# A two-layer gated attention and experts kernel: the second attention's tables loaded with x, its DRAM zeroed inside the first attention, its output weights prepared inside the slots, and a shorter row of steps for the normalization constants

## The chip, the cores and the metric

One Trainium2 chip, one of its cores. The metric is the device time of one execution in microseconds (us), median over several executions.

## The reference

The state `x` has 64 batches of 128 tokens by 128 features; the context `ctx_1024` has 64 batches of 77 tokens. Four stages are added to `x` in turn, each on a layer-normalized `x`:

```python
x = x + tanh(g_xattn[0]) * L0_xattn(ctx, ctx, layernorm(x))   # feature maps exp(z), exp(-z); 16 heads
x = x + tanh(g_ffn[0])   * L0_ffn(layernorm(x))               # 8 gated experts of width 336, routed
x = x + tanh(g_xattn[1]) * L1_xattn(layernorm(x), ctx, ctx)   # attention with relative key and value tables
x = x + tanh(g_ffn[1])   * L1_ffn(layernorm(x))               # 8 experts of width 256, top 2
# layernorm(x) = (x - mean) / sqrt(var + 1e-5)
# L1_xattn: q = x Wq + bq, k = c Wk + bk, v = c Wv + bv, 16 heads of 8
#   scores = (q k + q rel_key[q - k]) / sqrt(8); p = softmax(scores)
#   out = (p v + p rel_value[q - k]) Wo + bo
```

All of `x` stays in SBUF (`x_all`, 128 partitions by 64 batches by 128) from the load to the last stage.

## The kernel before

The program is a row of blocks, and all engines meet at a barrier between two blocks: the load of `x` (`load_x`, L129), normalization constants (`layernorm_constants`, L82), the first attention (`feature_attention`, L167), constants, router and scores, the first experts, constants (the third call), the second attention (`relative_attention`, L1384), constants, router, scores and the second experts.

`load_x`: SP issues four DMAs of 1 MB for `x`, then the small tables of both routers (L144). POOL first clears those router tables (L150). DVE takes `bn_stats` of every batch as its quarter lands (L164).

`layernorm_constants` turns the two half-row statistics of all 64 batches into mean, `1/sqrt(var + eps)` and, where asked, the shift `-mean * rstd`. It is called four times. DVE runs a chain in which `link` (L101 to L105) lets every operation wait for the one before it: seven operations (L108 to L116), of which the sixth releases the square root on ACT (L95), then the reciprocal (L118), four operations of one Newton step (L120 to L123) and the shift (L125).

Both attentions are software pipelines, and `slots` (L66) gives each engine the same slot numbers: the first and last slots are written out, the middle ones are a hardware loop over two parities. In a slot an engine runs a hand-ordered row of functions that belong to different batches, each with its own semaphore waits.

First attention, SP (L239 to L251): seven weight tables; then in slot n the DMA of batch n's context (`xc`, L246), which PE's `prep_z` (L269) needs. At slot 2, behind the context of batch 2, SP also issues the 20 DMAs of the first experts' weights (`stage_cuts`, L249, some 4 MB). Batch 3's context follows them in the same queue.

Second attention: SP loads eight tables (L1476), waits until POOL has cleared `q_pos` (L1761), and writes these zeros into the two DRAM buffers `queries` (L1479), because later only a diagonal pattern of them is written (L1485) and the whole is read back (L1492). SP waits until both have landed before its first slot.

DVE copies the identity into head order (`by_head_ident`, L1800), waits for the eight tables, and prepares: the selector and the split row bias (L1804 to L1812, six steps of `bias_split`), the output weights and bias times the gate (L1814, L1815; `weights_ready` 1 and 2), the masked key table (L1817), then the low part of the output weights and the output bias in rows (L1821 to L1831). The bias takes one product on PE (L1650). ACT first waits for the tables and for `weights_ready` 1 and rounds the output weights (L1661). Only then do the slots begin on PE and ACT, and on DVE after L1831. PE waits for `weights_ready` 3, `w_out_low`, `table_ready` and `bias_split` 6 ahead of its first slot; POOL waits for `weights_ready` 3.

The slots run from -4. Batch 0 comes up like this: ACT normalizes (L1693), PE transposes (L1522), ACT rounds (L1667), DVE makes the low part (`low_xn`, L1837), PE projects in slot -2 (L1526, L1542), ACT and DVE split the queries (L1684, L1686, L1845, L1847; the count `proj_low`), POOL spreads them over the heads (`mask_queries`, L1769), SP writes them to DRAM and reads them back, and PE computes scores (L1557, L1559).

## Time and profile before

| | us |
|---|---|
| median of 3 executions | 2190.94 (2188.76 to 2191.07) |
| the profiled execution | 2186.11 |
| its span in the profile | 2184.2 |
| load and first constants | 0 to 25.1 |
| first attention, to its last statistics | 25.65 to 466.3 |
| second constants to the end of the first experts | 467.2 to 1195.3 |
| third constants | 1195.6 to 1199.5 |
| second attention | 1199.97 to 1785.3 |
| fourth constants | 1785.6 to 1789.3 |
| second router and experts | 1789.8 to 2184.2 |

Busy time as a share of the span: PE 93%, DVE 87%, ACT 72%, POOL 72%. A timeline row gives the start, the length (for merged rows the stretch they cover), the engine ("SPq" is a DMA issue on SP, "PEld" a weight load), the line, the operation and the count; behind it, in brackets, how long the engine had been idle and what released it. The last column but two of a windows row is TensorE's granted clock (1.00 is 2.4 GHz, 0.50 is 1.2 GHz), the last two are the DMA engines' busy share and GB/s.

### The profile page before, as it was taken

The numbers are of one execution on the slowest core, as the hardware profiler recorded it, in microseconds if no ns is written. First come the engines' busy times: TensorE is split into PE (matmuls) and PEld (weight loads), VectorE is DVE, ScalarE is ACT, GpSimd is POOL, SyncE is SP. The second block draws the span as 40 slices with busy tenths as digits, with TensorE's granted clock in tenths as the row PEclk, the third lists the DMA queues.
The fourth block names the chain that finished last, engine by engine and source line by source line (L and its number), as shares of the span: only waits on it lengthen the run. The fifth ranks groups of instructions, "written<-read, shape, count | busy, mean of one in ns | idle before, by whom it ended". The sixth has DMA issues, their size and how long they took to land. (4 is left out here: it accounts for less than half of the span.)

```text
span 2184.2 us, 82970 instructions
## 1 busy us (share of the span) xinstructions
PE 2035.4 (93%) x28380; PEld 1568.6 (72%) x28380; DVE 1904.4 (87%) x4327; ACT 1570.4 (72%) x3516; POOL 1575.8 (72%) x1457
## 2 busy tenths in 40 slices
PE   3999999977999999999998799999999966999999
PEld 2788888854666666666665689999999944666666
DVE  5899999987888888888888689999999968888888
ACT  3788888875565655555555578888888756888887
POOL 1576777743666666666665789999999933888887
PEclk9999999987999999999999799999999978999999
DMA  5000000002432222222220455555555520000000
GB/s 155 14 6 7 6 7 6 7 2 74 102 90 82 78 86 82 82 85 83 79 84 16 85 81 89 82 89 82 89 83 89 83 60 1 15 10 14 10 14 15
DMA packets 476443, 121.41 MB, mean 56 GB/s; under 512 B 431879, under 2 KB 446855, under 8 KB 475604
## 3 DMA queue, kind: packets, MB, share of 16 engines
q1 hardware_dynamic: 476084, 120.41, 25.2%
q8 instruction: 42, 0.69, 0.1%
q14 instruction: 29, 0.24, 0.0%
q10 hardware_dynamic: 288, 0.07, 0.0%
HBM read 106.51 MB, written 13.89 MB: 55 GB/s over the span
## 5 line engine op out<-in xcount | busy, mean ns | idle before, releaser
L1220 POOL TENSOR_TENSOR f_low<-f_hidden,f_high 128x512 f16<-128x512 f32 x336 | 442.4, 1322 | 217.9 <-ACT f_high L1152 216.0
L1178 DVE TENSOR_TENSOR f_hidden<-f_hidden,f_share 128x512 f32<-128x512 f32 x336 | 374.2, 1114 | 0.0
L1367 POOL TENSOR_TENSOR f_low<-f_hidden,f_high 128x512 f16<-128x512 f32 x256 | 296.7, 1160 | 74.1 <-ACT f_high L1310 74.1
L1158 ACT ACTIVATE f_act_out<-f_gate 128x512 f32<-128x512 f32 x336 | 200.5, 597 | 193.2 <-PE f_gate L1122 193.1
L1201 DVE SCALAR_TENSOR_TENSOR f_hidden<-f_up,f_act_out 128x512 f32<-128x512 f32 x336 | 229.8, 684 | 83.2 <-PE f_up L1122 51.0
L1152 ACT ACTIVATE f_high<-f_hidden 128x512 f16<-128x512 f32 x336 | 210.5, 626 | 72.9 <-DVE f_hidden L1178 71.6
L1132 PE MATMUL f_y<-w_high,f_high 128*128 128x128 f16 x1344 | 243.3, 219 | 2.0 <-POOL f_low L1220 2.0
L1769 POOL TENSOR_TENSOR a_q_head_high<-a_q_t_high,a_head_mask 128x2048 f16<-128x2048 f16 x64 | 233.0, 3641 | 16.3 <-DVE a_q_t_low L1847 8.0
L1132 PE MATMUL f_y<-w_high,f_low 128*128 128x128 f16 x1344 | 243.4, 219 | 0.0
L1132 PE MATMUL f_y<-w_low,f_high 128*128 128x128 f16 x1344 | 243.3, 219 | 0.0
L1769 POOL TENSOR_TENSOR a_q_head_low<-a_q_t_low,a_head_mask 128x2048 f16<-128x2048 f16 x64 | 233.0, 3641 | 0.0
L1353 DVE SCALAR_TENSOR_TENSOR f_hidden<-f_in,f_act_out 128x512 f32<-128x512 f32 x256 | 175.8, 687 | 49.7 <-ACT f_act_out L1317 49.7
L1317 ACT ACTIVATE f_act_out<-f_in 128x512 f32<-128x512 f32 x256 | 152.9, 597 | 65.4 <-PE f_in L1279 59.6
L1557 PE MATMUL a_score<-a_k_t_high,a_q_head_high 128*128 128x77 f16 x1024 | 186.4, 201 | 4.8 <-POOL a_q_head_low L1769 2.8
L1291 PE MATMUL f_y<-w_high,f_high 128*128 128x128 f16 x1024 | 184.8, 219 | 2.3 <-DVE x_all L1331 0.6
L1559 PE MATMUL a_score<-table_low,a_q_pos 128*128 128x77 f16 x1024 | 186.7, 202 | 0.0
L1559 PE MATMUL a_score<-table_high,a_q_pos 128*128 128x77 f16 x1024 | 186.6, 202 | 0.0
L1557 PE MATMUL a_score<-a_k_t_high,a_q_head_low 128*128 128x77 f16 x1024 | 186.4, 201 | 0.0
L1557 PE MATMUL a_score<-a_k_t_low,a_q_head_high 128*128 128x77 f16 x1024 | 186.2, 201 | 0.0
L1291 PE MATMUL f_y<-w_high,f_low 128*128 128x128 f16 x1024 | 184.6, 219 | 0.0
L1291 PE MATMUL f_y<-w_low,f_high 128*128 128x128 f16 x1024 | 184.6, 219 | 0.0
L1878 DVE TENSOR_TENSOR a_prob_t_low<-a_trans,a_prob_t_high 77x512 f16<-77x512 f32 x256 | 166.6, 670 | 15.1 <-ACT a_prob_t_high L1706 14.3
(280 smaller groups left out, 8171.1 us busy)
## 6 DMA issues: line engine op xcount, KB each, us to landing
f_share<-expert_shares SPq DMA_DIRECT2D x128, 256.0 KB, 3.1
a_q_pos<-queries SPq DMA_DIRECT2D x64, 512.0 KB
f_share<-expert_shares SPq DMA_DIRECT2D x128, 128.0 KB, 3.0
relative_values<-a_rel_all SPq DMA_DIRECT2D x512, 8.0 KB
x_all<-in_x SPq DMA_DIRECT2D x4, 1024.0 KB, 8.0
f_share<-expert_shares SPq DMA_DIRECT2D x128, 32.0 KB, 1.8
queries<-a_q_parts SPq DMA_DIRECT2D x64, 64.0 KB, 3.1
a_rel<-relative_values SPq DMA_DIRECT2D x64, 64.0 KB, 2.1
```

The costliest lines, as they stand in the source:

```text
L1132: mm = nc.tensor.matmul(dst, h[r][:, own], w_down[part][:, m, :], start=(m == 0 and t == 0 and k == 0), stop=(m == M - 1 and k == 2), skip ...
L1152: nc.scalar.activation(high[r][:, :], hidden[r][:, :], ACT.Copy).then_inc(high_ready, 1)
L1158: nc.scalar.activation(act_out[m % RING][:, :], gate_ps[m % BANKS][:, :], ACT.Silu, scale=1.0 / WSCALE).then_inc(act_ready, 1)
L1178: nc.vector.tensor_tensor(hidden[r][:, :], hidden[r][:, :], share[k][:, :, :].rearrange("p t q -> p (t q)"), ALU.mult).then_inc(scaled, 1)
L1201: nc.vector.scalar_tensor_tensor(out=hidden[r][:, :], in0=up_ps[m % BANKS][:, :], scalar=1.0 / WSCALE, in1=act_out[r][:, :], op0=ALU.mult, ...
L1220: nc.gpsimd.tensor_tensor(low[r][:, :], hidden[r][:, :], high[r][:, :], ALU.subtract).then_inc(low_ready, 1)
L1291: mm = nc.tensor.matmul(dst, h[m % RING][:, own], w_down[part][:, m, :], start=(c == 0 and t == 0 and k == 0), stop=(c == per - 1 and k == 2),
L1353: nc.vector.scalar_tensor_tensor(out=dst, in0=src, scalar=scalar, in1=a, op0=op, op1=ALU.mult).then_inc(hidden_ready, 1)
L1367: nc.gpsimd.tensor_tensor(low[k][:, :], hidden[k][:, :], high[k][:, :], ALU.subtract).then_inc(low_ready, 1)
L1557: nc.tensor.matmul(dst, q[:, QC * g:QC * (g + 1), :], t[:, :], start=(k == 0), stop=False)
L1559: mm = nc.tensor.matmul(dst, q_pos[p][:, g, :], key_table[k][:, 0, window], start=False, stop=(k == 1))
L1769: nc.gpsimd.tensor_tensor(q_head[p][k][:, :, :], q_t[p][k][:, :].unsqueeze(2).broadcast_to([P, P, NH]), head_mask[:, :].unsqueeze(1).broad ...
```

## The change

1. `layernorm_constants`: operations that do not need each other no longer wait for each other; eps is added together with the square; the Newton step takes three operations in place of four.
2. A class `AttentionTables` is allocated with the router tables. Its eight tables are loaded by SP at the end of `load_x`; POOL clears one row `empty_row` (256 bytes a partition) there.
3. The two DRAM buffers are zeroed in the first attention: SP issues both DMAs at slot 2, behind the experts' weights, with `empty_row` repeated 16 times as their source. `q_pos` is no longer cleared.
4. In the second attention all engines wait for the long-landed tables only. The product for the output bias goes to PE's slot -2 (its head), the rounded output weights to ACT's slot -2 (its head), and the seven DVE operations L1821 to L1831 to the head of DVE's slot -1. PE's waits move to the first place that needs each.

```diff
 layernorm_constants, DVE
-  link(mean = half1 + half4); link(diff = half1 - half4); link(var = half2 + half5)
-  link(diff = (diff * 0.25) * diff); link(var = var / D + diff); link(var = var + EPS)   # 6: releases ACT
-  link(mean = mean * 0.5)
+  diff = half1 - half4; var = half2 + half5; mean = half1 + half4
+  dve.wait_ge(step, 1)
+  diff = (diff * 0.25 * D) * diff
+  dve.wait_ge(step, 4)
+  var = (var + EPS * D) + diff
+  dve.wait_ge(step, 5)
+  var = var * (1.0 / D)                                                                  # 6: releases ACT
+  mean = mean * 0.5
   dve.wait_ge(root, 1)
   rstd = reciprocal(sd)
-  link(newton = rstd * rstd); link(newton = newton * var); link(newton = newton * -0.5 + 1.5)
-  link(rstd = rstd * newton)
+  newton = (rstd * -0.5) * rstd; newton = newton * var; rstd = (newton + 1.5) * rstd      # each waits
```

(The block above writes the operations in short; the ones below are the diff's own lines.)

```diff
 load_x
-                sp.wait_ge(cleared, sum(len(r.zeros) for r in routers))
-                for r in routers:
+                sp.wait_ge(cleared, sum(len(r.zeros) for r in (*routers, attention)))
+                for r in (*routers, attention):
                     for t, src in r.loads:
                         sp.dma_start(t, src).then_inc(r.loaded, 16)
 feature_attention, SP
                     if isinstance(n, int) and n == 2:
                         for dst, src in stage_cuts:
                             sp.dma_start(dst, src).then_inc(stage_in, 16)
+                        empty = attention.empty_row[:, :].unsqueeze(1).broadcast_to([P, QG, QC * NH])
+                        for dst in attention.q_read:
+                            sp.dma_start(dst, empty).then_inc(attention.emptied, 16)
 relative_attention, SP
-                for t, src in WEIGHTS:
-                    sp.dma_start(t[:, :], io[src]).then_inc(weights_in, 16)
-                sp.wait_ge(cleared, 1)
-                for p in range(2):
-                    sp.dma_start(q_read[p], q_pos[p][:, :, :]).then_inc(q_zeroed, 16)
-                sp.wait_ge(q_zeroed, 32)
+                sp.wait_ge(attention.emptied, 32)
 relative_attention, PE
+                        if isinstance(n, int) and n == -2:     # in project
+                            pe.wait_ge(bias_split, 6)
+                    if isinstance(n, int) and n == -2:         # head of slot
+                        output_bias()
-                pe.wait_ge(weights_ready, 2)
-                nc.tensor.matmul(fin_ps[:, 0:D], b_v[:, :], w_o[:, :], start=True, stop=True).then_inc(bias_ready, 1)
-                pe.wait_ge(weights_ready, 3)
-                pe.wait_ge(w_out_low, 1)
-                pe.wait_ge(table_ready, 1)
-                pe.wait_ge(bias_split, 6)
+                def output_bias():
+                    pe.wait_ge(weights_ready, 2)
+                    nc.tensor.matmul(fin_ps[:, 0:D], b_v[:, :], w_o[:, :], start=True, stop=True).then_inc(bias_ready, 1)
+                pe.wait_ge(attention.loaded, 16 * len(attention.loads))
                 slots(pe, FIRST, LO, HI, LAST, slot)
 relative_attention, ACT
-                act.wait_ge(weights_in, 16 * len(WEIGHTS))
-                act.wait_ge(weights_ready, 1)
-                nc.scalar.activation(w_out[0][:, :], w_o[:, :], ACT.Copy).then_inc(w_out_high, 1)
+                act.wait_ge(attention.loaded, 16 * len(attention.loads))
+                    if isinstance(n, int) and n == -2:         # head of slot
+                        high_output()
 relative_attention, POOL
-                    last = nc.gpsimd.memset(q_pos[p][:, :, :], 0.0)
-                last.then_inc(cleared, 1)
-                pool.wait_ge(weights_ready, 3)
+                pool.wait_ge(attention.loaded, 16 * len(attention.loads))
 relative_attention, DVE
-                dve.wait_ge(weights_in, 16 * len(WEIGHTS))
+                dve.wait_ge(attention.loaded, 16 * len(attention.loads))
...
+                    if isinstance(n, int) and n == -1:         # head of slot; L1821 to L1831
+                        output_tables()
```

The remaining waits of PE go to the first users: `table_ready` to `scores(0)`, `weights_ready` 3 to `mix_turn(0)`, `w_out_low` to `fin_project(0)`. The DRAM tensors and their access patterns move into `AttentionTables` unchanged.

## Rows read from the trace of the kernel before

**Rows 1.** Windows: the loop of the second attention, busy us by engine, clock, DMA share, GB/s

```profile
1219.00:1780.00 561.00, 542.50 (x12711) 517.11 (x12711) 500.48 (x1397) 444.74 (x1267) 509.37 (x253) 0.98 0.52 82
```

**Rows 2.** Timeline, third call of layernorm_constants: start us, us, engine, line, operation

```profile
1195.60 1.28 ACT L95 ACT_TABLE_LOAD   x1 [4.89 <-PEq L1097]
1195.63 0.27 DVE L108 TENSOR_TENSOR mean<-stats 128x64 f32<-128x64 f32 x1 [0.30 <-PEq L1097]
...
1196.55 0.23 DVE L111 SCALAR_TENSOR_TENSOR ln_diff<-ln_diff 128x64 f32<-128x64 f32 x1
...
1197.07 0.20 DVE L115 TENSOR_SCALAR ln_var<-ln_var 128x64 f32<-128x64 f32 x1
...
1197.30 0.26 ACT L95 ACTIVATE ln_sd<-ln_var 128x64 f32<-128x64 f32 x1 [0.41 <-DVE ln_var L115]
...
1198.25 0.23 DVE L120 TENSOR_TENSOR ln_newton<-rstd 128x64 f32<-128x64 f32 x1
...
1199.00 0.22 DVE L123 TENSOR_TENSOR rstd<-rstd,ln_newton 128x64 f32<-128x64 f32 x1
```

**Rows 3.** Timeline, DVE at the start of the first attention: two operations without a wait

```profile
30.59 0.43 DVE L498 TENSOR_TENSOR a_fm_w<-a_w_rep,a_w_sign 128x256 f32<-128x256 f32 x1 [5.44 <-DMA a_fc_w<-in_fc_w]
30.93 0.15 DVE L502 TENSOR_TENSOR a_own_mask<-a_head_mask 128x4 f32<-128x4 f32 x1
```

**Rows 4.** Timeline, start of the second attention, all engines

```profile
1200.01 4.20 DVE L1800 COPY a_by_head_ident<-ident 128x128 f32<-128x128 f32 x1 [0.54 <-PEq L91]
...
1200.28 1.80 POOL L1761 MEMSET a_q_pos<- 128x2048 f16 x1
...
1202.33 1.80 POOL L1761 MEMSET a_q_pos<- 128x2048 f16 x1
...
1205.31 0.29 DVE L1804 TENSOR_TENSOR a_sel<-ident 128x128 f16<-128x128 f32 x1 [1.09 <-DMA a_high_rows<-in_high_rows]
...
1207.09 0.27 DVE L1817 TENSOR_SCALAR table_low<-table_low,a_high_rows 128x197 f16<-128x197 f16 x1
...
1207.22 0.79 PE L1650 MATMUL a_mix<-a_w_o,a_b_v 128*128 128x128 f32 x2 [13.53 <-DVE a_b_o L1815]
1207.29 0.86 ACT L1693 ACTIVATE a_xn<-x_all,xn_shift,rstd 128x128 f32<-128x128 f32 x2
...
1208.40 0.47 PE L1522 MATMUL a_prep<-ident,a_xn 128*128 128x128 f32 x1 [0.38 <-DVE a_b_o L1823]
...
1209.55 0.28 DVE L1837 TENSOR_TENSOR a_xt_low<-a_prep,a_xt_high 128x128 f16<-128x128 f32 x1
...
1209.90 0.29 PE L1526 MATMUL a_prep<-a_xt_high,table_high 128*128 128x128 f16 x1 [1.02 <-DVE a_xt_low L1837]
```

**Rows 5.** Timeline, POOL and DVE in the first slots of the second attention

```profile
1212.13 3.64 POOL L1769 TENSOR_TENSOR a_q_head_high<-a_q_t_high,a_head_mask 128x2048 f16<-128x2048 f16 x1 [8.00 <-DVE a_q_t_low L1847]
...
1215.28 0.29 DVE L1845 TENSOR_TENSOR a_q_parts<-a_prep,a_q_parts 128x128 f16<-128x128 f32 x1 [2.07 <-ACT a_q_t_high L1686]
```

**Rows 6.** Timeline of the first attention, SP's queue and PE after the pieces of line 249

```profile
57.40 0.36 SPq L246 DMA_DIRECT2D a_xc<-in_ctx  x1
...
59.34 1.71 PE L269 MATMUL a_prep<-a_xc,a_fm_w 128*128 128x205 f32 x4 [7.25 <-DMA a_xc<-in_ctx]
```

**Rows 7.** Line 1479, the two DMAs of zeros: issue ns (min, median, max), landing us

```profile
L1479 SPq DMA_DIRECT2D queries<-a_q_pos x2: 381/920/1458, 1204.2 to 1204.6; - x2
...
DMA to landing us min/median/max: 3.9/4.9/5.8
```

**Rows 8.** DMA issues of the first 100 us: KB each, median us to landing

```profile
r_w_rows<-in_r_router SPq DMA_DIRECT2D x2, 4.0 KB, 7.2
...
a_w_rep<-in_fm_w SPq DMA_DIRECT2D x1, 4.0 KB, 1.6
```

**Rows 9.** Timeline, the load stage: the statistics on DVE, the last DMA issue on SP

```profile
8.54 12.47 DVE L164 BATCH_NORM_STATS2 stats<-x_all 128x6 f32<-128x128 f32 x64 [4.63 <-DMA x_all<-in_x]
...
11.72 0.44 SPq L144 DMA_DIRECT2D r_w_rows<-in_r_router  x1
```

More of the change, by code:

```diff
@@ L98, in _ @@
             def _(dve):
-                done = 0
-                def link(ins):
-                    nonlocal done
-                    done += 1
-                    ins.then_inc(step, 1)
-                    dve.wait_ge(step, done)
-                half = [stats[:, :, k] for k in range(6)]
-                link(nc.vector.tensor_tensor(mean[:, :], half[1], half[4], ALU.add))
-                link(nc.vector.tensor_tensor(diff[:, :], half[1], half[4], ALU.subtract))
-                link(nc.vector.tensor_tensor(var[:, :], half[2], half[5], ALU.add))
@@ new lines, in _ @@
+                nc.vector.tensor_tensor(diff[:, :], half[1], half[4], ALU.subtract).then_inc(step, 1)
+                nc.vector.tensor_tensor(var[:, :], half[2], half[5], ALU.add).then_inc(step, 1)
+                nc.vector.tensor_tensor(mean[:, :], half[1], half[4], ALU.add).then_inc(step, 1)
+                dve.wait_ge(step, 1)
+                nc.vector.scalar_tensor_tensor(out=diff[:, :], in0=diff[:, :], scalar=0.25 * D, in1=diff[:, :],
+                                               op0=ALU.mult, op1=ALU.mult).then_inc(step, 1)
@@ new lines, in _ @@
+                dve.wait_ge(step, 4)
+                nc.vector.scalar_tensor_tensor(out=var[:, :], in0=var[:, :], scalar=EPS * D, in1=diff[:, :],
+                                               op0=ALU.add, op1=ALU.add).then_inc(step, 1)
+                dve.wait_ge(step, 5)
+                nc.vector.tensor_scalar(var[:, :], var[:, :], 1.0 / D, None, ALU.mult).then_inc(step, 1)
+                nc.vector.tensor_scalar(mean[:, :], mean[:, :], 0.5, None, ALU.mult).then_inc(step, 1)
+                dve.wait_ge(root, 1)
@@ new lines, in _ @@
+                nc.vector.reciprocal(rstd[:, :], sd[:, :]).then_inc(step, 1)
+                dve.wait_ge(step, 8)
+                nc.vector.scalar_tensor_tensor(out=newton[:, :], in0=rstd[:, :], scalar=-0.5, in1=rstd[:, :],
+                                               op0=ALU.mult, op1=ALU.mult).then_inc(step, 1)
+                dve.wait_ge(step, 9)
+                nc.vector.tensor_tensor(newton[:, :], newton[:, :], var[:, :], ALU.mult).then_inc(step, 1)
+                dve.wait_ge(step, 10)
@@ L131, in load_x @@
+def load_x(nc, B, x, x_all, stats, routers, attention):
     G = 4
@@ L147, in _ @@
             def _(pool):
-                for r in routers:
+                for r in (*routers, attention):
                     for t in r.zeros:
@@ L1381, in _, with relative_attention @@
                     sp.wait_ge(x_stored, 16 * G)
-def relative_attention(nc, B, io, x_all, stats, mean, rstd, xn_shift, ident, gates, ctx_t, tables, q_dram, r_dram):
+def relative_attention(nc, B, io, x_all, stats, mean, rstd, xn_shift, ident, gates, ctx_t, tables, attention):
     with ExitStack() as ctx:
@@ L1620, in fin_project @@
                         if isinstance(n, int) and n == 0:
+                            pe.wait_ge(w_out_low, 1)
                             pe.wait_ge(out_bias, 4)
```

98 lines of the change are left out of this document (54 added, 44 removed).

## Prediction

> **What bounds the kernel now.** I began with the page. Its chain of waits, followed back from the end, stays within the last experts stage and says nothing of the code that changes, so I went by stages. The windows of the second attention's loop show the first thing: PE is busy 542 of 561 us at a granted clock of 0.98 of full speed, the full level [rows 1]. A loop like that isn't touched by this change; only what stands before it is. Between two blocks every engine meets the others, so each microsecond taken out of a serial opening, or put into it, shows in the total one for one. The timelines of three such places carry the forecast: the constants [rows 2], the opening of the second attention [rows 4, 5] and one stall in the first attention, where the change puts its new DMAs [rows 6].
>
> The sum is made against the profiled execution: 2186.11 us, a span of 2184.2 and 1.9 around it. The median of the runs is 4.8 us above that; I carry a difference over to the median unchanged. About 0.2%, or 4.4 us, is what a measurement of this kernel can tell from no change.
>
> **Part 1, the constants (four calls).** To the start of the square root the old chain takes 1197.30 - 1195.63 = 1.67 us; an operation on the strided statistics lasts 0.27, a scalar_tensor_tensor 0.23, a tensor_scalar 0.20, and a waited link adds 0.03 [rows 2]. What an unwaited successor gains is seen elsewhere [rows 3]: the second operation starts at 30.93, while the first ends at 31.02, an overlap of 0.09. The new chain then has starts at 0, 0.18, 0.36 (the three sums), 0.54 (the square), 0.54 + 0.23 + 0.03 = 0.80, 1.06 (the scaling), and releases ACT at 1.06 + 0.20 + 0.03 = 1.29. ACT's table load is done at 1195.60 + 1.28, which is 1.25 after the chain's start, and stays just hidden; it is the floor of this gain. Gain 0.38. The Newton step takes 0.97 us for four operations (1198.25 to 1199.22) and 0.75 for three (3 x 0.23 + 2 x 0.03): 0.22. A call gains 0.60, four calls **2.4 us**. The halving of the mean runs beside the square root, and costs nothing; without that cover it would be 0.20. Bounds: 0.9 us (only the dropped operation counts) to 2.6 (the table load is the floor: 0.42 + 0.22).
>
> The Trainium skill, page VectorE: DVE Perf Modes, section The DRAIN you can't avoid, speaks against this part: a chain of copies took as long with a semaphore behind each as with one behind the last. By that rule only the dropped Newton operation would count, and the sum would be 1.5 us smaller. The overlap [rows 3] speaks against the rule, on one pair; it is a rival below.
>
> **Part 2, the load stage.** POOL clears one more small row, and SP issues eight DMAs more, at about 0.45 us each (its last one takes 0.44) [rows 9]. They stand behind x in the queue, and DVE's statistics (8.54 to 21.01, without a gap after the first quarter) set the end [rows 9]. I cost them at nothing: the router's issues end at 12.16 us, the new ones near 16, five before the cover ends. If some moved past 21 us, SP would enter the barrier late by that much.
>
> **Part 3, the opening of the second attention.** Before, DVE's copy of the identity takes 4.20 us and ends at 1204.21; POOL's last memset of q_pos ends at 1202.33 + 1.80 = 1204.13 [rows 4]. A 128x128 operation of DVE otherwise lasts 0.27 to 0.29 [rows 4], so I read the copy as held until POOL is through. What remains on POOL is the filling of value, four memsets of which the first two fit between the block's start and 1200.28, where the first q_pos memset starts [rows 4]; both pairs end some 0.65 us after the block's start. So the copy ends 0.8 us after it, instead of 4.24.
>
> The Trainium skill, page SBUF - State Buffer, section Who interferes with whom, has this as a rule: a copy of VectorE in its two-port mode and a GpSimd instruction block one another for a whole instruction. By it the copy falls with the memsets; without it 3.4 us of this part's gain would be missing. The one row agrees, and cannot show more.
>
> Now times from the block's start (1199.97 before). The eight tables are there, so the 1.09 us for the last of them goes. DVE's preparation from L1804 to the start of L1817 took 1207.09 - 1205.31 = 1.78, and the next operation can start 0.19 later: low_xn(0) at 0.8 + 1.97 = 2.8. ACT no longer waits for the weights: it normalizes at once (two in 0.86), and from PE's transposition to low_xn(0) it took 1209.55 - 1208.40 = 1.15 at most, so batch 0 is there by 2.1, hidden beside DVE. PE's output-bias product, 0.79 us long and until now released at 1207.22, is ready at 0.8 + 1.91 = 2.7 and stands ahead of the projection in slot -2, so that begins near 3.4, where it began 1209.90 - 1199.97 = 9.93 after the start. **Gain 6.5 us.** Behind it the row is as before: POOL's first mask, which starts at 1212.13 on the projection's low part, and everything that hangs on it [rows 5]. The DMA path through DRAM starts from the same projection, so it moves along. The zeros themselves had landed at 1210.4 [rows 7], before SP's first write could start, and cost nothing there beyond their memset.
>
> DVE's seven moved operations (1.8 us with links) stand at the head of slot -1. There DVE sits idle 2.07 us before 1215.28 [rows 5], so they fit; what would be late, if not, is the split of the second projection, with POOL's masks of 3.64 us each in front of it as a further cover. ACT's rounding (0.3) waits for a product DVE has finished by then. I take both as nothing. Bounds of the part: 3.1 us (the copy keeps its 4.2) to 7.0 (the copy isn't held at all).
>
> **Part 4, the zeros in the first attention.** SP issues batch 3's context at 57.40, after 20 weight DMAs; PE waits 7.25 us for it and starts at 59.34 [rows 6]. At that point SP is to issue two DMAs of 512 KB in 256-byte pieces first. In the second attention the same two took 0.38 and 1.46 us to issue, and the second landed 5.8 us after its issue, in all 1204.16 to 1210.4 = 6.25 us [rows 7]. The context goes into the same queue behind them. That a queue keeps its order is seen in the router's 4 KB table: 7.2 us to land behind x, where a table of the same size takes 1.6 in an empty queue [rows 8]. So the context lands soon after 57.40 + 6.25, and PE starts near 64.1: **a loss of 4.8 us**. PE, ACT, DVE and POOL all stand in that stall, so nothing hides it, and the pipeline behind has no slack to win it back. Bounds: 1.9 us (only the issues delay it, the context overtakes the zeros) to 9 (the writes go at about half the speed beside other traffic, or because the source is one row repeated).
>
> **Sum.** -2.4 - 6.5 + 4.8 = -4.1: the profiled 2186.11 becomes 2182.0, and the median of 2190.94 becomes **2186.8 us**, 0.19% less. What was gained at one opening is mostly spent in an older stall.
>
> **The rivals.** (a) The context isn't held by the zeros. For it: 38.5 KB is small, and the DMA engines are lightly used at 57 us. Against: the router table behind x [rows 8]. Time: -2.4 - 6.5 + 1.9 = -7.0, 2183.9 us. Chance 0.12. (b) The copy of the identity is slow for its own, reordered reading, and stays at 4.2. For: no second row of it exists. Against: its end within 0.1 us of POOL's. Then -2.4 - 3.1 + 4.8 = -0.7: 2190.2. Chance 0.12. (c) Waits between operations are free, as the rule above says: -0.9 - 6.5 + 4.8 = -2.6: 2188.3. Chance 0.07. (d) Slower: the zeroing is slow in the first attention. Its place is SP's queue between 57.4 us and batch 3's context. Each further microsecond costs one; the kernel is slower than before from a stall longer by 8.9 us, that is zeros that need 10.4 in place of 6.25, and at twice their time the sum is -2.4 - 6.5 + 11.0 = +2.1: 2193.0. For: the source is another one, and this runs behind 4 MB of weights. Against: the number and size of the pieces are the same. Chance 0.06. (e) The change doesn't do what it says at the second attention: something with a time of its own, such as the copy through DRAM, holds the first scores, and half of the head start is lost: 2190. Chance 0.05.
>
> **How the numbers follow.** My own case has 0.58, and its own range is 2185.3 to 2188.3, so it straddles the 2186.6 below which the kernel counts as faster: I give 0.26 of it to faster and 0.32 to the same. With (a) all faster, (b), (c) and (e) the same, and half of (d) slower: faster 0.39, same 0.58, slower 0.03; for the spread of the medians themselves (2.3 us over three runs) I move a little outwards: 0.40, 0.55, 0.05. The range takes in (a) below and (b) above with some margin: 2183.2 to 2190.8.
>
> **What would show it.** Right: PE's stall before its fourth product of line 269 grows from 7.25 to about 12 us; DVE's copy of the identity lasts under 1 us; the first projection of the second attention starts 3.4 us after its block, and POOL's first mask 5.7 instead of 12.2; each call of the constants is 0.6 us shorter. Wrong: a stall that stays near 9 us (a), a copy that stays at 4.2 (b), calls shorter by 0.2 only (c), a stall over 16 us (d), or a first score that moves by much less than the first mask (e).

## The result, and the profile after

The changed kernel takes 2177.4 us (2174.02 to 2182.85, six executions), the kernel before beside it 2189.85 (2187.81 to 2193.77, six): a ratio of 0.9946 (95%: 0.9934 to 0.9958), 12.4 us less. The forecast had 4.1 less, and its range (2183.2 to 2190.8) ended above the result. The profiled execution took 2174.02 us with a span of 2172.1, 12.1 less than the one before.

**The constants.** The timeline of the third call, DVE and ACT (compare [rows 2]):

```profile
1194.29 1.28 ACT L95 ACT_TABLE_LOAD   x1 [4.27 <-PEq L1119]
1194.32 0.27 DVE L100 TENSOR_TENSOR ln_diff<-stats 128x64 f32<-128x64 f32 x1 [0.30 <-PEq L1119]
1194.51 0.26 DVE L101 TENSOR_TENSOR ln_var<-stats 128x64 f32<-128x64 f32 x1
1194.69 0.26 DVE L102 TENSOR_TENSOR mean<-stats 128x64 f32<-128x64 f32 x1
1194.87 0.22 DVE L104 SCALAR_TENSOR_TENSOR ln_diff<-ln_diff 128x64 f32<-128x64 f32 x1
...
1195.61 0.26 ACT L95 ACTIVATE ln_sd<-ln_var 128x64 f32<-128x64 f32 x1
...
1196.49 0.22 DVE L115 SCALAR_TENSOR_TENSOR ln_newton<-rstd 128x64 f32<-128x64 f32 x1
...
1197.01 0.23 DVE L120 SCALAR_TENSOR_TENSOR rstd<-ln_newton,rstd 128x64 f32<-128x64 f32 x1
```

The starts 0, 0.19, 0.37, 0.55 and the root at 1.29 are the ones that were forecast, to 0.01. From the start of the last Newton operation to the first operation of the next block it is 0.80 us (1197.01 to 1197.81), where it was 1.0 (1199.00 to 1200.01, [rows 2, 4]). That piece was not forecast.

**The opening of the second attention.** The timeline of all engines from the block's start at 1197.8 (compare [rows 4]):

```profile
1197.79 0.88 ACT L1714 ACTIVATE a_xn<-x_all,xn_shift,rstd 128x128 f32<-128x128 f32 x2 [1.92 <-PEq L91]
1197.81 0.40 DVE L1821 COPY a_by_head_ident<-ident 128x128 f32<-128x128 f32 x1 [0.32 <-PEq L91]
...
1197.99 0.28 DVE L1825 TENSOR_TENSOR a_sel<-ident 128x128 f16<-128x128 f32 x1
...
1200.08 0.79 PE L1671 MATMUL a_mix<-a_w_o,a_b_v 128*128 128x128 f32 x2 [1.20 <-DVE a_b_o L1836]
1200.12 0.28 DVE L1859 TENSOR_TENSOR a_xt_low<-a_prep,a_xt_high 128x128 f16<-128x128 f32 x1
...
1200.66 0.31 PE L1538 MATMUL a_prep<-a_xt_high,table_high 128*128 128x128 f16 x1
...
1202.92 3.64 POOL L1790 TENSOR_TENSOR a_q_head_high<-a_q_t_high,a_head_mask 128x2048 f16<-128x2048 f16 x1 [4.41 <-DVE a_q_t_low L1869]
```

The copy of the identity fell from 4.20 to 0.40 us. The first projection starts 2.85 after the block does (forecast 3.4, before 9.93), POOL's first mask 5.11 after it (forecast 5.7, before 12.12 by the block's first operation at 1200.01). What follows was forecast as free, and isn't. The same timeline, DVE and POOL (compare [rows 5]):

```profile
1203.92 2.79 DVE L1843 TENSOR_TENSOR a_w_out_low<-a_w_o,a_w_out_high 128x128 f16<-128x128 f32 x1
1206.51 3.68 POOL L1790 TENSOR_TENSOR a_q_head_low<-a_q_t_low,a_head_mask 128x2048 f16<-128x2048 f16 x1
1206.62 0.27 DVE L1845 TENSOR_TENSOR a_b_o<-a_b_o,a_mix 128x128 f32<-128x128 f32 x1
1206.93 3.35 DVE L1847 CAST a_out_rows<-a_b_o 128x128 f16<-128x128 f32 x1
1210.31 0.29 DVE L1849 TENSOR_TENSOR a_b_o<-a_b_o,a_out_rows 128x128 f32<-128x128 f32 x1
...
1211.43 0.34 DVE L1869 SCALAR_TENSOR_TENSOR a_q_t_low<-a_prep,a_b_q,a_q_t_high 128x128 f16<-128x128 f32 x1
...
1212.06 3.64 POOL L1790 TENSOR_TENSOR a_q_head_high<-a_q_t_high,a_head_mask 128x2048 f16<-128x2048 f16 x1 [1.86 <-DVE a_k_t_low L1873]
```

The moved DVE operations (six, by the trace and the code, not seven) last 7.4 us (1203.92 to 1211.31), not 1.8. Two of them, of 128 elements a partition, take 2.79 and 3.35 us. They end 0.15 us behind POOL's first mask (1206.56) and 0.09 behind its second (1210.19). The operation between them, which takes one of its inputs from PSUM (`a_mix`), runs beside the second mask in 0.27. So the split of the next projection comes late, and POOL stands 1.86 us before its third mask: 14.25 us after the block's start instead of 12.3 (5.11 and the 7.19 that lay between the first mask and the third before). PE's first score of this block moves with it: 14.56 us after the start, where it was 19.40.

**The stall in the first attention.** Timeline, SP's queue and PE (compare [rows 6]), and the view of line 251, the zeros (compare [rows 7]; issue in ns, landing in us):

```profile
55.65 1.42 SPq L251 DMA_DIRECT2D queries<-a_empty_row  x2
57.18 2.94 SPq L245 DMA_DIRECT2D a_xc<-in_ctx  x2
61.17 1.36 PE L271 MATMUL a_prep<-a_xc,a_fm_w 128*128 128x205 f32 x3 [10.15 <-DMA a_xc<-in_ctx]
```

```profile
L251 SPq DMA_DIRECT2D queries<-a_empty_row x2: 424/688/952, 55.6 to 56.1; - x2
...
DMA to landing us min/median/max: 3.3/4.0/4.7
```

The stall grew from 7.25 to 10.15 us, by 2.9 instead of 4.8.

**The loop.** Windows of the second attention's loop, as in [rows 1]:

```profile
1212.00:1773.00 561.00, 540.67 (x12713) 516.74 (x12714) 501.57 (x1399) 450.50 (x1270) 509.46 (x254) 0.98 0.52 82
```

In this view, which starts at POOL's third mask as the one of [rows 1] does, it looks as before. But the sum of the pieces so far is -3.7 (four calls, 0.88 to 0.99 each from the traces), -7.0 (first mask), +1.9 (third mask), +2.9 (stall) = **-5.9 us**, about half of 12.4. In the two profiled executions the other 6.2 us lie where the change was thought to touch nothing: 3.8 between the third mask and the end of the second attention (562.2 us for 566.0), 2.2 in the block of the first experts (722.1 for 724.3), 0.3 in the rest. The experts' block takes 722.1 to 725.8 us over all seventeen traces; it is 722.2 in c1_constants_only and 725.8 in a_tables_slot2 and e_memsets_back, which build on the change, so its 2.2 are credited to no edit. The runs below look for the rest.

### The profile page after: what moved, and what is told of

Same layout as the page of the kernel before. It is cut to its first block and busy times, and to the rows that moved or that the text cites. A ratio compares the mean times of both kernels' runs of the same rounds, so it can differ in the third digit from the quotient of the medians.

```text
span 2172.1 us, 82958 instructions
## 1 busy us (share of the span) xinstructions
PE 2031.3 (94%) x28380; PEld 1567.1 (72%) x28380; DVE 1903.7 (88%) x4323; ACT 1573.5 (72%) x3516; POOL 1571.2 (72%) x1456
```

## The experiments

Each set of experiments had its own executions of the kernel before on the same chip; their medians were 2195.7 (c1, a, b, e), 2198.92 (r_changed_again, f1, f2, g), 2199.86 (r_shares_first, h1, c2, d) and 2194.83 (h2, h3, z1), so times are compared within a set only.

### The constants

**c1_constants_only:** the kernel before with the new `layernorm_constants` (the first part of the change's diff, whole) alone.

```diff
-                link(nc.vector.tensor_tensor(diff[:, :], half[1], half[4], ALU.subtract))
...
+                nc.vector.tensor_tensor(diff[:, :], half[1], half[4], ALU.subtract).then_inc(step, 1)
...
```

> The kernel before with the new layernorm_constants alone. By the two traces each call, from its first operation on DVE to the first work of the next block, went from 4.17-4.35 to 3.18-3.45 us, 0.9 to 1.0 less, where my steps held 0.6. If the whole of that belongs to this function, the kernel is 3.6 to 4.0 us faster than before (2189.9 to about 2186.1) and the gap between DVE's last operation and the next block's first is 0.27 instead of 0.51 us. Rival: the shorter gap comes from another part of the change (what the next block begins with); then the gaps stay at 0.5 and the gain is 2.4 to 2.8 us.

2192.19 us (2188.37 to 2198.81, 12) against 2195.7: ratio 0.9984 (0.9975 to 0.9994), -3.5 us. In its trace the calls, from the first operation to the next block's first one, take 8.40, 3.24, 3.49 and 3.23 us, where they took 9.28, 4.13, 4.38 and 4.22: -3.65 together. The gain is 0.9 a call and not 0.6.

How much of the first call's 0.9 reaches the end of the kernel is open. It brings PE's first context product forward, from 32.87 to 33.13 us (the eight traces with the old constants) to 32.20 (c1) and 32.29 (c2, below). But the stall for batch 3's context is then 8.37 and 8.23 us long, and PE goes on at 59.20 and 59.33, where it went on at 59.34 to 60.29 after stalls of 7.25 to 8.67.

**c2_last_wait:** c1, and DVE waits for its last operation before it enters the barrier, as the old chain did.

```diff
                                                    op0=ALU.mult, op1=ALU.mult).then_inc(step, 1)
+                dve.wait_ge(step, 11 if shift is None else 12)
```

> The kernel before with the new constants and one wait more: DVE waits for its own last operation at the end of each call, as the old chain did. Theory: the old chain's last wait kept DVE from the block's end, so the gap between its last operation and the next block's first grows from 0.32 back to 0.5 us, and a call takes 0.2 us more (3.4 instead of 3.23 for the second and fourth). Rival: the wait costs nothing there and the call stays at 3.23.

Calls of 8.50, 3.44, 3.71 and 3.45 us: 0.1 to 0.2 more than in c1. One execution took 2196.84, which decides nothing by itself. The timelines of DVE show the place; c1 first, c2 second:

```profile
1195.64 0.23 DVE L124 SCALAR_TENSOR_TENSOR xn_shift<-mean,rstd 128x64 f32<-128x64 f32 x1
1196.19 4.21 DVE L1799 COPY a_by_head_ident<-ident 128x128 f32<-128x128 f32 x1 [0.32 <-PEq L91]
```

```profile
1199.65 0.23 DVE L124 SCALAR_TENSOR_TENSOR xn_shift<-mean,rstd 128x64 f32<-128x64 f32 x1
1200.42 4.20 DVE L1800 COPY a_by_head_ident<-ident 128x128 f32<-128x128 f32 x1 [0.54 <-PEq L91]
```

With the wait the barrier starts when the shift has ended, and DVE is idle for 0.54 us, as in [rows 4]; without it the sequencer walks into the barrier while the shift runs, and the idle time is 0.32. The wait accounts for the missing 0.2 of a call: the forecast looked for unwaited links inside the chain and not at its end. The remaining 0.07 lies between the root and the first Newton step (0.95 before, 0.88 after).

### The opening

**e_memsets_back:** the changed kernel with POOL's clearing of `q_pos` put back; nothing needs it.

```diff
 relative_attention, POOL
+                    last = nc.gpsimd.memset(q_pos[p][:, :, :], 0.0)
+                last.then_inc(cleared, 1)
...
 relative_attention, SP
                 sp.wait_ge(attention.emptied, 32)
+                sp.wait_ge(cleared, 1)
```

> The changed kernel with POOL's two memsets of q_pos put back at the start of the second attention (SP waits for them). Theory: DVE's copy of the identity is held by POOL's memsets, so it lasts about 4.2 us again (0.40 in the changed kernel), and POOL's first mask starts 3.4 to 4 us later than the 5.15 us after the block's start; the span grows by about as much. Rival: the copy was slow for something else at that place (the tables' DMAs into SBUF or the DMAs of zeros); then it stays near 0.4 us.

```profile
1202.19 4.20 DVE L1825 COPY a_by_head_ident<-ident 128x128 f32<-128x128 f32 x1 [0.32 <-PEq L91]
...
1204.52 1.80 POOL L1786 MEMSET a_q_pos<- 128x2048 f16 x1
...
1210.80 3.63 POOL L1794 TENSOR_TENSOR a_q_head_high<-a_q_t_high,a_head_mask 128x2048 f16<-128x2048 f16 x1 [4.48 <-DVE a_q_t_low L1873]
```

The copy takes 4.20 us again and ends at 1206.39, 0.07 us behind the second memset, and the first mask starts 8.61 us after the block instead of 5.11. So 3.5 us of the opening came from the memsets, by way of a copy on another engine. The other half of the 7.0 is what is left for the tables, which are there, and for the products taken out of the way; no run separates these two. The copy isn't slow by itself: rival (b) falls. (One execution, 2185.5 us; the verdict rests on the trace.)

**a_tables_slot2:** the moved DVE operations one slot earlier, before POOL's masks begin.

```diff
-                    if isinstance(n, int) and n == -1:
+                    if isinstance(n, int) and n == -2:
                         output_tables()
```

> The changed kernel with the seven DVE operations of output_tables at the head of slot -2 instead of slot -1. In the changed kernel they take 7.3 us (1203.92 to 1211.31) beside POOL's first two masks, and POOL then idles 1.9 us. Theory: DVE and POOL block one another there; in slot -2, before POOL's first mask, the seven take about 1.9 us, DVE's idle 1.8 us covers most of it, the first mask starts 0.3 to 0.6 us later, the 1.9 us idle of POOL goes, and the kernel is 1.3 to 1.6 us faster than the changed one. Rival: the seven are slow by themselves (a chain with waits on ACT and PE); then they take over 5 us in slot -2 too, the first mask comes 4 us later and the kernel is 2 us slower than the changed one.

```profile
1204.87 0.28 DVE L1843 TENSOR_TENSOR a_w_out_low<-a_w_o,a_w_out_high 128x128 f16<-128x128 f32 x1
...
1205.78 0.23 DVE L1847 CAST a_out_rows<-a_b_o 128x128 f16<-128x128 f32 x1
...
1206.69 0.35 DVE L1853 SCALAR_TENSOR_TENSOR a_out_rows<-a_out_rows,ident,a_b_o 128x128 f16<-128x128 f16 x1
1207.65 3.63 POOL L1790 TENSOR_TENSOR a_q_head_high<-a_q_t_high,a_head_mask 128x2048 f16<-128x2048 f16 x1 [4.59 <-DVE a_q_t_low L1869]
...
1211.24 3.63 POOL L1790 TENSOR_TENSOR a_q_head_low<-a_q_t_low,a_head_mask 128x2048 f16<-128x2048 f16 x1
```

The same operations, with no mask beside them, take 0.28 and 0.23 us, all six 2.2. So they aren't slow by themselves. The first mask starts 0.18 us later (5.29), but the third at 12.47 after the block's start instead of 14.25: the collision cost 1.8 us. In total 2182.1 us (2181.66 to 2184.25, 5), ratio 0.9942 (0.9929 to 0.9954); the 1.8 us can't be told from the changed kernel's 0.9946 that way, so its size rests on the trace.

### The zeros

**b_zeros_in_load:** the changed kernel with its two DMAs of zeros behind the small tables in the load stage, where DVE's statistics run on to 20.8 us.

```diff
 load_x, SP
...
+                for dst in attention.q_read:
+                    sp.dma_start(dst, empty).then_inc(attention.emptied, 16)
 feature_attention, SP, slot 2
...
-                        for dst in attention.q_read:
-                            sp.dma_start(dst, empty).then_inc(attention.emptied, 16)
```

> The changed kernel with the two zeroing DMAs at the end of SP's queue in the load stage instead of slot 2 of the first attention. They are issued at about 16 us and should have landed by 21, when DVE's statistics end. Theory: PE's stall for batch 3's context falls from 10.2 back to 7.3 us, the kernel is 2.9 us faster than the changed one (near 2174.5). Rival: the zeros hold up the seven weight tables of the first attention instead (issued from 24.6 us), then DVE's wait for them grows from 5.2 us and a part of the 2.9 is lost.

```profile
57.25 1.70 PE L271 MATMUL a_prep<-a_xc,a_fm_w 128*128 128x205 f32 x4 [6.15 <-DMA a_xc<-in_ctx]
```

2176.88 us (2174.2 to 2180.4, 5), ratio 0.9922 (0.9909 to 0.9935). The stall is 6.15 us where the changed kernel had 10.15: the zeros cost 4.0 where they stand. Against the kernel before (7.25) it is 2.9 only, since without them this stall is 1.1 shorter than it was. The traces show where: SP is through with the 20 weight DMAs at 55.3 us in b and at 55.7 to 56.4 in the five traces of the change with its zeros in place, but at 57.1 to 58.4 in the ten traces of the kernel before and its variants, c1 and c2 among them. Neither the constants (c1) nor, below, the SBUF placement (f2), the DRAM placement (f1, r_shares_first) or the separate row (z1) makes this difference; what does stays open. The stall itself spreads: 7.25 to 8.67 us in the eight traces with the old constants and the old zeros (8.2 and 8.4 with the new constants), 10.15 to 11.24 in the five with the change's zeros. The 7.25 and the 10.15 are the lowest of their groups, and by the others the zeros cost up to 5.1. The rival in this expectation, that the zeros hold up the first attention's weight tables instead, has no support: the first call, which ends with the wait for them, takes 8.44 us (8.40 in the changed kernel).

**d_row_source** and **z1_own_row:** the kernel before; in d its zeros are written from the first row of each `q_pos`, repeated, in z1 from one separate small row that POOL clears besides (with the SBUF placement of f2, below).

```diff
-                    sp.dma_start(q_read[p], q_pos[p][:, :, :]).then_inc(q_zeroed, 16)
+                    sp.dma_start(q_read[p], q_pos[p][:, 0:1, :].broadcast_to([QC * QB, QG, QC * NH])).then_inc(q_zeroed, 16)   # d
+                    sp.dma_start(q_read[p], early[8][:, :].unsqueeze(1).broadcast_to([P, QG, QC * NH])).then_inc(q_zeroed, 16) # z1
```

> The kernel before with one edit: the two zeroing DMAs at the start of the second attention read one row of q_pos (256 bytes a partition), repeated 16 times, instead of all 4 KB of each partition. In the kernel before they moved 1 MB at about 210 GB/s and the second landed 6.25 us after the first issue; in the changed kernel, from the repeated row and in the first attention, at about 290 GB/s and 5 us. If the source makes the difference, they run at 290 GB/s here too and land 1.3 us sooner; if the place in the program does (DRAM, other traffic), they stay at 210.

> The kernel before with the zeros written, at the same place in the second attention, from a separate row of 256 bytes a partition (as in the changed kernel), where the row of q_pos repeated changed nothing (217 GB/s, second landing 5.8 us after its issue). If the separate, small source tensor is what makes 285 GB/s and 4.7 us, both show here; if the place in the program is, they stay at 217 and 5.8.

One execution each: 2198.64 and 2194.72 us, beside 2199.86 and 2194.83. The landings, in the view of the line: d 3.9/4.9/5.8 us, as before; z1:

```profile
L1478 SPq DMA_DIRECT2D queries<-a_empty_row x2: 380/692/1005, 1203.7 to 1204.1; - x2
...
DMA to landing us min/median/max: 3.3/4.0/4.7
```

So the second landing is 1.1 us sooner from the separate row, at both of these places: neither the repetition (d), nor the SBUF placement alone (f2, below: 3.9/4.9/5.8), nor the order of the DRAM tensors (r_shares_first, below, lands like the changed kernel) makes it. What it is about the separate row stays open. It is no fixed time either: in b, from the same row but at 16 us, the two land 5.3 and 6.6 us after their issue.

**g_all:** the changed kernel with a and b, and the 20 cuts of weights spread over slots 1 to 3.

```diff
-                    if isinstance(n, int) and n == 2:
-                        for dst, src in stage_cuts:
+                    if isinstance(n, int) and 1 <= n <= 3:
+                        for dst, src in stage_cuts[(0, 3, 9, len(stage_cuts))[n - 1]:(0, 3, 9, len(stage_cuts))[n]]:
...
```

> The changed kernel with output_tables at DVE's slot -2, the zeros written in the load stage, and the 20 weight DMAs of the first attention spread over SP's slots 1, 2 and 3 (3, 6 and 11 of them). The first two gave -1.8 and some -3 to -4.6 us. Spreading: batch 3's context then stands behind nine DMAs instead of twenty, is issued near 46 us instead of 55, and is there before PE wants it (50 us); the next context stands behind eleven small ones. PE's stall of 6.2 us shrinks to under 2. Together 8 to 11 us faster than the changed kernel. Rival: the weights hold up another context by as much (batch 2 or 4), and the spreading gives nothing; then 5 to 6 us.

Windows of all engines over 14 us of the first attention, the changed kernel (r_changed_again) first, g second:

```profile
48.00:62.00 14.00, 3.20 (x51) 2.54 (x47) 4.67 (x12) 4.49 (x11) 3.62 (x7) 0.78 0.81 190
```

```profile
48.00:62.00 14.00, 14.00 (x202) 11.47 (x198) 13.59 (x34) 12.75 (x32) 8.79 (x18) 1.00 0.09 20
```

The stall is gone: PE is busy 14.00 of 14 us instead of 3.20. The first attention takes 425.8 us. It takes 438.5 to 441.2 in the five traces of the change with its zeros in place, 433.9 in b, and 435.1 to 438.4 in the ten of the kernel before and its variants. The kernel takes **2169.5 us** (2167.5 to 2174.02, 4), ratio 0.9876 (0.9861 to 0.9891), and beats both. The cuts in one piece, and not the zeros, were the larger part of what the context waited for (6.15 us are left in b without the zeros).

The gain from b to g in this stage is 8.1 us, more than the 6.15 of the stall. The windows of b behind its stall show a place for the rest: PE had stood idle since 51.1, and when it goes on at 57.25 its granted clock is at the lower level, 0.50 (1.2 GHz), and back at 1.00 in the window from 62. In g it is 1.00 throughout. About 4 us of work at half the clock would lose about 2 us, by estimate from these windows.

```profile
57.00:60.00 3.00, 2.75 (x8) 1.68 (x8) 0.00 (x0) 0.95 (x2) 0.33 (x1) 0.50 0.11 16
60.00:62.00 2.00, 2.00 (x35) 1.78 (x34) 1.64 (x4) 0.39 (x2) 1.92 (x5) 0.78 0.00 0
```

The expectation was 8 to 11 us less than the changed kernel; beside r_changed_again it is 16.5. The two traces have it as 12.9 in the first attention, 1.8 at the third mask, 2.2 in the first experts (which no edit explains) and 0.9 in the rest. The expectation had counted the stall of 6.2 us alone, and not what comes behind it.

### The other half

**r_changed_again:** the changed kernel, unedited, beside the next two.

> The changed kernel once more, as the reference for the three that run beside it. Its pieces that the traces fix are: constants -3.7 us, opening of the second attention -5.1 us (counted to the fourth batch), stall in the first attention +2.8 us, together -6.0 us or 0.27%. The ratio measured at first was 0.9946, 6 us more than that. If the 6 us are real, the ratio is again 0.994 to 0.996; if they were chance, it is near 0.997.

2185.99 us (2185.12 to 2189.62, 5) against 2198.92, ratio 0.9951 (0.9937 to 0.9964): the 12 us aren't an accident of one set.

The change moves the two DRAM tensors `queries` and `relative_values` (and tables in SBUF) to an earlier place of allocation: by the order of allocation their addresses change, and nothing else does. (The traces show no addresses; the order is what the code fixes.) The next runs test this on the kernel before, part by part.

**f1_dram_first**, **f2_sbuf_first**, **h1_relative_first**, **h2_queries_first**, **h3_shift_256k**, and **r_shares_first**, which goes the other way on the changed kernel:

```diff
 f1, h1, h2: the kernel before; both DRAM tensors (f1), relative_values alone (h1), queries alone (h2) ahead of expert_shares
+        q_dram = [nc.dram_tensor(f"queries{p}", [QG * Q_PITCH], F16).ap() for p in range(2)]            # f1, h2
+        r_dram = [nc.dram_tensor(f"relative_values{p}", [P, D], F32).ap() for p in range(2)]            # f1, h1
         x_high = ctx.enter_context(nc.sbuf_tensor("x_high", [P, B // GB, GT], F16))
 f2: the kernel before; nine small SBUF tables of the second attention allocated there instead
+        early = [ctx.enter_context(nc.sbuf_tensor("a1_" + n, [P, w], d)) for n, w, d in (
...
 h3: the kernel before; expert_shares is twice as large, its second half unused: both tensors lie 256 KB further
-            s_dram = nc.dram_tensor("expert_shares", [NE, B * P], F32).ap()
+            s_dram = nc.dram_tensor("expert_shares", [2 * NE, B * P], F32).ap()[0:NE, :]
 r_shares_first: the changed kernel; expert_shares ahead of both again
+        s_dram = nc.dram_tensor("expert_shares", [NE, B * P], F32).ap()
         attention = AttentionTables(nc, ctx, io)
```

> The kernel before with one edit: the DRAM tensors queries and relative_values are allocated ahead of expert_shares, as in the changed kernel. Theory: they lie at other addresses there, and the loop of the second attention, in which ACT waits 45 to 60 us in total for relative values to come back from DRAM, runs 4 to 8 us faster (ratio 0.996 to 0.998). Rival: the place in DRAM does nothing; ratio 1.000.

> The kernel before with one edit: the nine small tables of the second attention are allocated in SBUF together with the router tables (still loaded where they were), so that everything behind them lies 2.4 KB further, as in the changed kernel. Theory: the shift of addresses makes a stage 4 to 8 us faster (ratio 0.996 to 0.998). Rival: no effect, ratio 1.000.

> The kernel before with only relative_values (two tensors of 64 KB) allocated ahead of expert_shares; queries stay behind. If the place of relative_values, on whose return ACT and POOL wait in the loop, is what counts, the ratio is 0.997 as with both moved. If the place of queries (two of 528 KB) counts, it is 1.000.

> The kernel before with only queries (two tensors of 528 KB) allocated ahead of expert_shares; relative_values stay where they were. With both moved the ratio was 0.9969, with relative_values alone 1.0035. If the place of queries makes the gain, the ratio is 0.996 to 0.998 here; if it takes both together, it is 1.000 or above.

> The kernel before with expert_shares allocated at twice its size (the second half unused), so that queries and relative_values both lie 256 KB further, their order and their distance unchanged. If any other address changes the loop of the second attention, and being first is nothing special, the ratio differs from 1.000 by 0.002 or more, either way, and the loop's time with it; if only what lies first is faster, it is 1.000.

> The changed kernel with one edit: expert_shares is allocated in DRAM ahead of queries and relative_values again, as in the kernel before. Theory: with that the 6 us go that the constants, the opening and the stall leave unexplained, and the ratio to the kernel before is 0.997 instead of 0.995. Rival: the order in DRAM helped the kernel before only, by chance; then the ratio stays at 0.995.

| kernel | us (n) | before beside it | ratio (95%) | second attention behind its third mask, us |
|---|---|---|---|---|
| f1_dram_first | 2191.61 (6) | 2198.92 | 0.9969 (0.9957 to 0.9981) | 570.3 |
| f2_sbuf_first | 2199.0 (11) | 2198.92 | 0.9998 (0.9988 to 1.0008) | 574.3 |
| h1_relative_first | 2207.86 (5) | 2199.86 | 1.0035 (1.0021 to 1.0049) | 586.9 |
| h2_queries_first | 2189.3 (11) | 2194.83 | 0.9972 (0.9963 to 0.9981) | 568.1 |
| h3_shift_256k | 2189.93 (11) | 2194.83 | 0.9979 (0.997 to 0.9988) | 566.9 |
| r_shares_first | 2193.47 (6) | 2199.86 | 0.9964 (0.995 to 0.9977) | 578.2 |

The last column is the length, in each one's trace, from the start of POOL's third mask to the end of the last statistics, the same work in all of them. With the old placement it is 574.3 to 578.2 (f2, z1, d, c2, c1, r_shares_first: 574.3, 575.2, 576.6, 577.0, 577.5, 578.2). With the changed one it is 562.2 (the changed kernel's profile), and 564.4, 565.7, 568.1, 569.9, 570.2 in b, e, a, g and r_changed_again. f1, the kernel before with the changed placement, has 570.3. Six of the seven traces with the old placement lie above all seven with the changed one. The seventh doesn't: the profile that the forecast was made from shows 566.0 with the old placement. It is the execution at 2186.11 us, 4.8 below its median. So against that profile the loop is only 3.8 us shorter, and what the placement is worth must be read from the medians.

So the placement in DRAM is worth -6.8 us by f1 (0.31% of 2198.92; by the interval 4.2 to 9.5), the placement in SBUF nothing (f2). It isn't a matter of "early": `relative_values` alone costs 7.7 us (h1, where 0.997 or 1.000 was expected), `queries` alone gains (h2), and so does shifting both by 256 KB without any new order (h3). r_shares_first keeps all edits of the change and takes back the placement: its 7.9 us by the ratio (6.4 by the medians) agrees with the 5.9 counted above, within its interval. By the totals alone the taking back isn't shown, since its interval overlaps those of the changed kernel (0.9946 and 0.9951); its loop of 578.2 us, beside 562.2 and 570.2, is what shows it.

Where the time goes is seen at ACT's copy of `a_rel_all`, which waits for the read-back of `relative_values` from DRAM. The rows of that group in the same 500 us of five traces, from 1222 to 1722: h1, then two with the old placement (r_shares_first, z1), then h2 and h3. The columns are busy time, mean ns, and the idle time before it with its releasers:

```profile
L1718 ACT ACTIVATE a_rel_all<-a_rel 128x256 f32<-128x256 f32 x223 | 84.7, 380 | 73.2 <-DMA a_rel<-relative_values 67.2 <-PE a_rel L1579 3.8
```

```profile
L1739 ACT ACTIVATE a_rel_all<-a_rel 128x256 f32<-128x256 f32 x229 | 86.9, 380 | 65.6 <-DMA a_rel<-relative_values 62.8 <-PE a_rel L1595 0.5
```

```profile
L1717 ACT ACTIVATE a_rel_all<-a_rel 128x256 f32<-128x256 f32 x229 | 87.0, 380 | 63.1 <-DMA a_rel<-relative_values 58.4 <-PE a_rel L1578 2.8
```

```profile
L1718 ACT ACTIVATE a_rel_all<-a_rel 128x256 f32<-128x256 f32 x231 | 87.8, 380 | 55.2 <-DMA a_rel<-relative_values 48.3 <-PE a_rel L1579 5.4
```

```profile
L1718 ACT ACTIVATE a_rel_all<-a_rel 128x256 f32<-128x256 f32 x232 | 88.1, 380 | 53.9 <-DMA a_rel<-relative_values 48.2 <-PE a_rel L1579 4.3
```

The operation's own time is the same; its wait for the DMA goes from 67 over 63 and 58 to 48 us, and with it the number of steps done in the stretch rises from 223 over 229 to 232. Over all seventeen traces the wait goes roughly with the length of the loop, from 41.7 us (the changed kernel's profile) to 67.2 (h1), but not one to one: r_changed_again, whose loop is at 570.2 us, waits 56.7 us there, and g, at 569.9, waits 59.3, as long as kernels with loops of 577. In the same window PE, the busiest engine of the loop, waits for this copy 11.5 us in h1, 8.0 in r_shares_first and 4.5 in the changed kernel's profile, which is a part of the difference in their loops (587, 578 and 562) and not all of it. So this path is where the time is seen; that it is the whole cause isn't shown. Why an address matters, inside the DRAM or the DMA engines, stays open: the runs show that it does, in which loop, and by how much.

## Why the forecast was wrong

- **Part 1, mis-sized.** -0.60 a call was -0.9: -3.65 in place of -2.4 for the four. The chain to the root (0.38) and the Newton step (0.22) were right to 0.01. What was left out is the wait behind the chain's last operation, 0.2 us a call (c2), and 0.07 behind the root. The bound of 2.6 ("the table load is the floor") was wrong for the same reason: it looked only at the way to the root and the Newton step. Rival (c), waits between operations are free, falls: by it a call would have gained 0.2, and it gained 0.9. The rule behind it (the Trainium skill, page VectorE: DVE Perf Modes, section The DRAIN you can't avoid) is not what these chains show: operations of 0.27 us without a wait between them start 0.18 to 0.19 apart, and c1 against c2 measures the wait ahead of the barrier at 0.2 us.
- **Part 2, right.** The SP issues of the tables end at 15.9 us, DVE's statistics at 20.8; the stage is not longer (21.11 us to the first constants, 21.31 before).
- **Part 3, right in its gain, wrong in one cost.** First mask -7.0 against -6.5, but -5.1 at the third mask, from where the loop is counted: the forecast had the copy end 0.8 us after the block's start and the selector behind it, while the selector starts 0.18 after the copy does; so the bias product starts at 2.27 and the projection at 2.85. The copy did fall with the memsets. The step that failed in this part is "DVE's seven moved operations ... so they fit" (they are six). It priced them at the 1.8 us they took alone, and put them beside POOL's masks as "a further cover". Beside the masks the same operations take 7.4. The Trainium skill, page SBUF — State Buffer, section Who interferes with whom, which the forecast had used for the copy alone, says in the same place what happens here: a cast in its two-port mode and an operation with two SBUF inputs contend with a GpSimd instruction that reads SBUF, one with at most one SBUF input does not. By that rule the trace agrees for all three (3.35, 2.79 and 0.27 us). Price: 1.9 us from the forecast's pair of traces, 1.8 from a. The masks were no cover but the cause.
- **Part 4, right mechanism, mis-sized.** The context did wait behind the zeros: the second of them is issued near 56.1 and lands 4.7 us later, at 60.8, and PE starts at 61.17. So rival (a) falls. The term was 4.8, the zeros cost 4.0 (b; up to 5.1 by the other traces) and the stall grew by 2.9. It was made from landing times of zeros in another form (5.8; from the separate row they take 4.7), and it took the rest of the stall for unchanged, while SP was through with the weights ahead of the zeros 1.7 us sooner (55.65 for 57.40). Rival (d), slower zeros, lay on the wrong side of it.
- **The step that puts the result outside the range.** The forecast says of the second attention's loop: "A loop like that isn't touched by this change; only what stands before it is." That the DRAM tensors moved to another class was read as a change of text, and the loop has no term in the sum. It is worth 6.8 us by f1, more than the error of any term that the sum has.
- **The sum.** -3.7 - 7.0 + 1.9 + 2.9 = -5.9, and -6.8 for the placement: -12.7 against -12.4 measured. That they meet so closely is partly luck: the first four are read from one pair of traces, the last from the medians of another set, with an interval of 5 us; in that pair of traces the loop gave 3.8 and the experts 2.2. Without the placement the right terms would have given 2185.0, inside the range, and that too is a cancelling: the constants gave 1.3 more and the stall cost 1.9 less than forecast, the opening gave 1.4 less. Rival (e), a head start held up by something with a time of its own, has no support: the first score and the third mask moved by 4.8 and 5.1 us, less than the first mask's 7.0, and a shows the collision to be what held the third mask. In the chances, one sum is off: 0.26 and the 0.12 of (a) make 0.38 for faster, not 0.39, and the same gets 0.59, not 0.58.

## What to carry to other kernels

A moved allocation is part of a change: where every step of a loop goes through DRAM, test its place by itself (h3 did it with an unused 256 KB ahead of it) before crediting the edit. An operation that is moved must be priced beside its new neighbours: DVE operations of 0.3 us lasted 2.8 and 3.4 beside POOL's. And of a chain, count the way out of its last link too.

## What the runs showed of the hardware

- The place of two DRAM buffers, with the same DMAs on them, moved the kernel by -0.31% to +0.35% (f1, h1); a shift of 256 KB gave -0.21% (h3).
- Two DMAs of zeros, 512 KB each, landed in 3.3 and 4.7 us from a separate repeated row, and in 3.9 and 5.8 from the large tile or its own repeated row, at the same place (z1, d). From the separate row at another place it was 5.3 and 6.6 (b).
- DVE operations of 0.23 to 0.40 us beside POOL's masks or memsets lasted until POOL's operation ended: 2.79 and 3.35 us (the changed kernel; 0.28 and 0.23 in a), 4.20 (e; 0.40 without the memsets). One with one of its inputs in PSUM kept its 0.27.
- Behind a stall of 6.15 us PE's granted clock was 0.50, and 1.00 again 5 us later; the stage was 8.1 us longer than without the stall (b, g).
- A DVE wait for its own last operation ahead of a barrier lengthened DVE's idle time there from 0.32 to 0.54 us (c1, c2).
